# A recommendation MLP on one core: five gram units of chunk c+2 among layer 2 of chunk c, four spills and four gathers in place of one and sixteen

## The reference

```python
B, F, D = (2048, 27, 128)
dots = jnp.einsum('bfd,bgd->bfg', bottom_output, bottom_output)   # 27 x 27 per sample
pairs = dots[:, _TRIL_I, _TRIL_J]                                 # 351 of them
x = jnp.concatenate([bottom_mlp_output, pairs, pad], axis=1)      # 128 + 351 + 1 = 480
for w, b in ((w0, b0), (w1, b1), (w2, b2), (w3, b3)):             # 1024, 1024, 512, 256
    x = jax.nn.relu(x @ w.T + b)
return x @ w_out.T + b_out                                        # (2048, 1)
```

## Time and profile before

| | |
|---|---|
| median of 3 runs | 575.12 us (574.05 to 575.9) |
| profiled execution | 574.64 us, span of its profile 572.8 us |
| PE busy | 515.9 us (90%), 4073 matmuls |
| ACT, DVE, POOL busy | 334.4, 280.3, 262.5 us |
| DMA | 53.16 MB, mean 93 GB/s |
| SPq issues in the chain that ended last | 11%, spill 5%, gather's landing 2% |

### The profile page before, as it was taken

One profiled execution on the slowest core, in us unless ns is written; L12 is line 12 of the kernel. 1 busy time (PEld: TensorE's weight loads), 2 busy tenths in 40 slices (PEclk: granted clock), 3 DMA queues, 4 the chain that ended last, 5 costly groups with the idle time before them and its releaser, 6 DMA issues.

```text
span 572.8 us, 13768 instructions
## 1 busy us (share of the span) xinstructions
PE 515.9 (90%) x4073; PEld 506.0 (88%) x4073; DVE 280.3 (49%) x646; ACT 334.4 (58%) x844; POOL 262.5 (46%) x467
## 2 busy tenths in 40 slices
PE   6948977999999699969999699979999699979997
PEld 6938976999999699969999699969999699979996
DVE  2845875527751477326761377316761377412111
ACT  3635799527982389525992389625993289613112
POOL 2801266224773177513773167613774167623321
PEclk9987999899999799998999799998999799997999
DMA  9978572255722576127732577117732477110000
GB/s 243 281 259 197 135 117 46 79 92 79 112 35 78 85 119 109 62 40 121 116 50 75 84 116 114 62 32 122 117 57 74 77 126 110 46 41 1 1 1 1
DMA packets 263088, 53.16 MB, mean 93 GB/s; under 512 B 248950, under 2 KB 260246, under 8 KB 263062
## 3 DMA queue, kind: packets, MB, share of 16 engines
q1 hardware_dynamic: 262374, 52.66, 46.0%
q10 hardware_dynamic: 688, 0.16, 0.1%
HBM read 45.71 MB, written 7.09 MB: 92 GB/s over the span
## 4 chain that ended last, share of the span: by engine, by line
PE 66%; SPq 11%; DMA 8%; ACT 4%; issue 4%; POOL 3%; DVE 2%; ACTq 1%; POOLq 0%
PE acc L684 52%; SPq L378 11%; PE gram_ps L647 8%; DMA blocks<-grams 5%; ACT parts L775 3%; PE gram_ps L630 3%; DMA pairs<-blocks 2%; PE gram_ps L601 2%; ACT h_full L791 1%; PE turned_ps L606 1%; ACTq L378 1%; POOL parts L526 1%; POOL grams L533 1%; DMA early_rows<-in_r_bottom_output_dram 1%; DVE grams L888 1%
## 5 line engine op out<-in xcount | busy, mean ns | idle before, releaser
L684 PE MATMUL acc<-h_a,w_hi 128*128 128x256 f32 x1152 | 216.0, 286 | 1.4 <-POOL h_a L541 1.2
L684 PEld LDWEIGHTS acc<-h_a,w_hi 128*128 128x128 f32 x1152 | 180.2, 193 | 3.3 <-POOL h_a L541 2.8
L791 ACT ACTIVATE h_full<-acc,small_t 128x256 f32<-128x256 f32 x176 | 82.6, 473 | 148.7 <-PE acc L684 146.2
L541 POOL TENSOR_TENSOR h_a<-h_full,h_a 128x256 fp32r<-128x256 f32 x96 | 72.3, 753 | 204.0 <-DVE h_a L908 204.0
L684 PE MATMUL acc<-h_a,w_lo 128*128 128x256 f32 x576 | 163.2, 283 | 0.0
L775 ACT ACTIVATE parts<-gram_ps 27x216 f32<-27x216 f32 x448 | 152.4, 340 | 16.0 <-PE gram_ps L647 6.5
L684 PE MATMUL acc<-x,w_hi 128*128 128x256 f32 x512 | 109.9, 313 | 34.3 <-ACT h_full L791 25.8
L684 PEld LDWEIGHTS acc<-x,w_hi 128*128 128x128 f32 x512 | 91.3, 219 | 36.1 <-issue 22.8
L684 PEld LDWEIGHTS acc<-h_a,w_lo 128*128 128x128 f32 x576 | 110.8, 192 | 0.0
L684 PE MATMUL acc<-h_b,w_hi 128*128 128x256 f32 x512 | 94.2, 285 | 2.4 <-POOL h_b L541 2.4
L908 DVE CAST h_a<-h_full 128x256 fp32r<-128x256 f32 x96 | 29.2, 304 | 123.3 <-ACT h_full L791 123.3
(11 more groups left out here) (49 smaller groups left out, 390.0 us busy)
## 6 DMA issues: line engine op xcount, KB each, us to landing
rows<-in_r_bottom_output_dram SPq DMA_DIRECT2D x444, 64.0 KB, 2.0
blocks<-grams SPq DMA_DIRECT2D x8, 864.0 KB, 3.5
w_raw<-in_L_rec_w_dram SPq DMA_DIRECT2D x6, 1024.0 KB, 7.5
early_rows<-in_r_bottom_output_dram SPq DMA_DIRECT2D x12, 224.0 KB, 6.0
stage_pairs<-in_L_rec_w_dram SPq DMA_DIRECT2D x1, 1408.0 KB, 9.5
w_raw<-in_L_rec_w_dram SPq DMA_DIRECT2D x2, 512.0 KB, 8.9
mlp_rows<-r_bottom_mlp_output_dram SPq DMA_DIRECT2D x8, 128.0 KB, 2.2
pairs<-blocks SPq DMA_DIRECT2D x32, 31.5 KB
```

What stands on the lines that cost most here:

```text
L541: nc.gpsimd.tensor_tensor(h[:, m, 1, :], h_full[:, slot % 2, :], h[:, m, 0, :].bitcast(F32), ALU.subtract).then_inc(split_done, 1)
L684: last = nc.tensor.matmul(acc_slot(slot), weight(wp, layer, m, k), in_tile(layer, k, xp), start=(k == 0 and n == 0), stop=(k == K_TILES[la ...
L791: nc.scalar.activation(h_full[:, slot % 2, :], acc_slot(slot), ACT.Relu, bias=small_t[:, slot:slot + 1]).then_inc(drained, 1)
```

## The change

- A hook comes every 18 products instead of 15 in all chunks but chunk 0. A chunk's own list holds units 5 to 18 (14 hooks, the last at product 252) of chunk c+1, and in layer 2, at products 306, 324, 342, 360 and 378, hooks 0 to 4 of chunk c+2 (five row turns, four `xt`, two grams, one sum). Chunk 0 has these five at its hooks 49, 52, 55, 58 and 61. Chunk 6 has none ahead, so it leaves the loop and is written out.
- SP loads rows of chunk c+2's units 0 to 3 before the spill and of units 4 to 8 after the gather.
- `blocks` in DRAM is laid out by feature pair with a chunk's 256 samples in a row: the spill is four DMAs (one per sample group, 32 x 27 runs of 256 B), the gather four DMAs with runs of 1 KB.
- In the start-up SP issues two of the spills and ACT two, ahead of the bottom network's step; each issues two gathers.
- In chunk 0 the bottom network's products (k = 0) of tiles 0 to 5 come first, with tiles 2 to 5 in the banks of `turned_ps` and `gram_ps`. Their 18 products count for the hooks, so weight groups 9, 10 and 11 come among them. Tiles 4 and 5 wait for all eight groups of layer 0. Weight groups 9 to 24 use two banks of `gram_ps` instead of four.
- `weighted` has a tensor of its own, and two waits around `low_t` go.

```diff
-HOOK, FIRST_HOOK = 15, 6
+HOOK, FIRST_HOOK = 18, 6
+AHEAD, AHEAD_HOOK = 5, 49
-OUT_HOOK = 2
+OUT_HOOK, EARLY_TILES = 2, 6
...
-    steps.append(("mlp",))
+    steps += [("spill",), ("mlp",)]
...
+    for n in range(AHEAD):
+        hooks[AHEAD_HOOK + 3 * n] += unit_steps(n, 2)
     return hooks
...
+def hooks_of(now, ahead):
+    hooks = [unit_steps(n, 1) for n in range(AHEAD, UNIT_HOOKS)] if now else []
+    if ahead:
+        hooks += [[] for _ in range(len(hooks), 3 * TILE0[2] // HOOK)] + [unit_steps(n, 2) for n in range(AHEAD)]
+    return hooks
...
+    if first:
+        for m in range(EARLY_TILES):
+            products(0, m, 0, 1)
...
+            products(layer, m, 1 if first and layer == 0 and m < EARLY_TILES else 0, K_TILES[layer])
...
-        blocks = nc.dram_tensor("blocks", (GROUP, QUAD, FEATS, RUN), F32).ap()
+        blocks = nc.dram_tensor("blocks", (QUAD, FEATS, CHUNK), F32).ap()
...
+        def acc_slot(c, slot):
+            if isinstance(c, int) and c == 0 and 2 <= slot < EARLY_TILES:
+
+                return (turned_ps if slot < 4 else gram_ps)[:, slot - 2, 0:CHUNK]
             return acc[:, slot % ACC_RING, 0:CHUNK]
...
+            among = EARLY_TILES // 3 if BEFORE_CHUNK <= n < LATE_WEIGHTS else GRAM_RING * GRAM_BANKS
+            return gram_ps[:, n % among, :]
...
+        def spill_quad(engine, s):
+
+            engine.dma_start(blocks[:, :, s * RUN:(s + 1) * RUN], grams[QUAD * s:QUAD * (s + 1)]).then_inc(spilled, 16)
+
         def gather_piece(engine, f, nf, nk, q):
 
-            for s in range(GROUP):
-                src = bass.AP(blocks.tensor, (s * QUAD * FEATS + (FEATS + 1) * f + 1) * RUN,
-                              [[(FEATS + 1) * RUN, nf], [RUN, nk], [1, RUN]])
-                engine.dma_start(pairs[q % P:q % P + nf * nk, q // P, s * RUN:(s + 1) * RUN], src).then_inc(gathered[q // P], 16)
+            src = bass.AP(blocks.tensor, ((FEATS + 1) * f + 1) * CHUNK, [[(FEATS + 1) * CHUNK, nf], [CHUNK, nk], [1, CHUNK]])
+            engine.dma_start(pairs[q % P:q % P + nf * nk, q // P], src).then_inc(gathered[q // P], 16)
...
-                for u in range(ROWS_RING, UNITS):
+                start = isinstance(c, int) and c == 0
+                for u in range(ROWS_RING if start else ROWS_RING + AHEAD, UNITS):
                     load_rows(c + 1, u)
...
+                more = not (isinstance(c, int) and c == CHUNKS - 2)
+                if more:
+                    for u in range(ROWS_RING):
+                        load_rows(c + 2, u)
                 spill(c + 1)
                 gather(c + 1)
-                if not (isinstance(c, int) and c == CHUNKS - 2):
-                    for u in range(ROWS_RING):
+                if more:
+                    for u in range(ROWS_RING, ROWS_RING + AHEAD):
                         load_rows(c + 2, u)
...
+                elif BEFORE_CHUNK <= n < LATE_WEIGHTS:
+
+                    pe.wait_ge(w_done, max(n - 1, BEFORE_CHUNK))
...
-                        pe.wait_ge(w_done, groups_for(layer, m))
+                        pe.wait_ge(w_done, W0_GROUPS if layer == 0 and m >= 4 else groups_for(layer, m))
...
+                elif step[0] == "spill":
+                    act.wait_ge(grams_done, UNITS)
+                    act.wait_ge(early_moved, UNITS)
+                    for s in (2, 3):
+                        spill_quad(nc.scalar, s)
...
-                if u == 0 and not (isinstance(d, int) and d < 2):
-
-                    dve.wait_ge(summed_done, d - 1)
...
-                    dve.wait_ge(grams_done, (c + (1 if ends else 2)) * UNITS)
```

More of the change, by code:

```diff
@@ L111, with unit_steps @@
 assert len({q + i * d for _, n, q, d in ROW_RUNS for i in range(n)}) == PAIRS
-def unit_steps(n):
+def unit_steps(n, ahead):
     steps, g = [], n - 1 - XT_LAG
     if n < UNITS:
-        steps.append(("raw", n))
+        steps.append(("raw", ahead, n))
     if 1 <= n <= UNITS:
-        steps.append(("turn", n - 1))
+        steps.append(("turn", ahead, n - 1))
     if g >= 1:
-        steps.append(("sum", g - 1))
+        steps.append(("sum", ahead, g - 1))
     if g >= 0:
-        steps.append(("gram", g))
+        steps.append(("gram", ahead, g))
     if g == UNITS - 1:
-        steps.append(("sum", g))
+        steps.append(("sum", ahead, g))
     return steps
@@ L154, in first_hooks @@
     places = [FIRST_UNIT + 2 * i for i in range(4)] + [FIRST_UNIT + 8 + 4 * i // 3 for i in range(UNIT_HOOKS - 4)]
-    hooks = [[] for _ in range(LATE_HOOK + W_GROUPS - LATE_WEIGHTS)]
+    hooks = [[] for _ in range(3 * sum(K_TILES[n] * M_TILES[n] for n in range(3)) // FIRST_HOOK)]
     for n in range(BEFORE_CHUNK, LATE_WEIGHTS):
@@ L158, in first_hooks @@
     for u, place in enumerate(places):
-        hooks[place] += unit_steps(u)
+        hooks[place] += unit_steps(u, 1)
     for n in range(LATE_WEIGHTS, W_GROUPS):
@@ L162, in first_hooks, with chunk_steps, products @@
     assert places[-1] < LATE_HOOK
-    return hooks
-def chunk_steps(gram, first=False):
+    for n in range(AHEAD):
+        hooks[AHEAD_HOOK + 3 * n] += unit_steps(n, 2)
+    return hooks
+def hooks_of(now, ahead):
[3 more added lines that the diff above has]
+    return hooks
+def chunk_steps(now, ahead, first):
     steps, done = [], 0
-    hooks = first_hooks() if first else [unit_steps(u) for u in range(UNIT_HOOKS)] if gram else []
+    hooks = first_hooks() if first else hooks_of(now, ahead)
     every = FIRST_HOOK if first else HOOK
     hooks.reverse()
+    def products(layer, m, k, k1):
+        nonlocal done
+        while k < k1:
+            n = k1 - k
+            n = min(n, (every - done % every) // 3)
+            steps.append(("mm", layer, m, k, k + n))
+            k += n
+            done += 3 * n
+            if done % every == 0 and hooks:
+                steps.extend(hooks.pop())
+            if done == OUT_HOOK * every:
+                steps.append(("out",))
+    if first:
+        for m in range(EARLY_TILES):
+            products(0, m, 0, 1)
     for layer in range(3):
         for m in range(M_TILES[layer]):
-            if (layer, m) == (2, 2) and gram:
-                assert not hooks
+            if (layer, m) == (2, 2) and now:
                 steps.append(("mlp",))
[L180 to L193, removed]
+            products(layer, m, 1 if first and layer == 0 and m < EARLY_TILES else 0, K_TILES[layer])
+    assert not any(hooks)
+    if now:
         steps.append(("pairs",))
@@ L196, in chunk_steps, with steps_of @@
     return steps
+def steps_of(c):
+    fixed = isinstance(c, int)
+    return chunk_steps(not (fixed and c == CHUNKS - 1), not (fixed and c >= CHUNKS - 2), fixed and c == 0)
 def dlrm_program(nc, x, x_mlp, w0, b0, w1, b1, w2, b2, w3, b3, w_out, b_out, y):
@@ L544, in chunk @@
             def chunk(c):
-                ends = isinstance(c, int) and c == CHUNKS - 1
-                for step in chunk_steps(not ends, isinstance(c, int) and c == 0):
+                for step in steps_of(c):
                     if step[0] == "mm":
@@ L724, in _ @@
             chunk(0)
-            with pe.Fori(1, CHUNKS - 1) as c:
+            with pe.Fori(1, CHUNKS - 2) as c:
                 chunk(c)
+            chunk(CHUNKS - 2)
             chunk(CHUNKS - 1)
```

62 lines of the change are left out of this document (32 added, 30 removed).

## The result

| | before | changed |
|---|---|---|
| median | 574.89 us (574.05 to 575.9) | 532.16 us (530.62 to 536.04) |
| profiled execution, its span | 574.64, 572.8 us | 532.41, 530.6 us |
| chunk to chunk, chunks 2 to 5 | 64.9 us | 58.5 us |
| start of chunk 1 | 128.7 us | 126.5 us |

What follows compares the result with a forecast made beforehand. PE was taken as the bound nearly everywhere, standing still at chunk ends. 574.64 - 39.5 + 2.5 - 3.0 - 4.4 + 0.3 = 530.5, 531.0 on the median's footing; forecast range 526 to 536 (0.52).

Steps and rivals of the forecast that it cites:

- The handover: Ends of chunks 1 to 6: PE's pause and half clock both go, 6.6 us each, -39.5 us in all.
- the stalls' +0.5 and -0.5: Per chunk: layer 3's stall grows by 0.5 us, the stall and refill before layer 2 go, 0.5 us.
- The spill's price: Writing grams to DRAM at a chunk's end: 3.7 us transfer plus 1.3 is 5.0 us; range 3.5 to 8.8.
- The doubling: Spill, rival A: short writes at double price, 8.8 us, total 541.8; chance 0.28 together with rival of ACT-bound layers.
- Unit 4's rows: SP's queue behind the gather: rows land at 51.8, DVE must start by 54.2; 2.4 us slack, high spill 1.4 late.
- a sign of being wrong: Layer 2: DVE idle before raw with the rows as releaser would show the prediction wrong; no size given.
- Layer 3: Late last drain and split behind ACT's parts copies: stall about 0.7 us instead of 0.2, +2.5 us over five chunks.
- The stall between layers 1 and 2: PE's 0.41 us wait for POOL's last split of layer 1 goes with its refill, -3.0 us over six chunks.
- ACT held in layer 0: Layer 0 with full hooks: ACT needs 14.2 us for PE's 14.2; taken as 0, bounds 0 to 1 us each.
- The start-up: Before chunk 0's main work: PE restarts at 40.7 instead of 44.40, with three more products behind it, -4.4 us.
- The slower rival: Rival D, at spill: SP stands in it, gather and unit 4 wait; slower than before from 13.4 us; chance 0.04.
- The rival's formula: Spill of s us: each handover late by s - 7.4, start-up by s - 5.0; s = 14.3 gives 581.

Runs made afterwards that it cites:

- the gathers alone: The changed kernel with hooks 15 products apart and no units among layer 2, new layout and early products kept; 534.2 us, ratio 0.930.
- the drawing forward alone: The changed kernel with the old layout of `blocks`, one spill and 16 gathers; 571.7 us, ratio 0.995.
- unit 4's rows first: The changed kernel with SP issuing unit 4's rows of chunk c+2 between spill and gather, not in chunk 0; 532.0 us, ratio 0.928.
- four units: The changed kernel with four units among layer 2 instead of five; 530.0 us, ratio 0.925.
- hooks of 15: The changed kernel with hooks 15 products apart instead of 18, five units ahead kept; 534.3 us, ratio 0.930.
- the two spread-out versions: The changed kernel with four units ahead and chunk 0's units spaced three hooks in two units, or five in three; 525.1 us (0.914) and 526.2 us (0.916).

## Why the prediction was right, step by step

**The handover.** It was nearly the whole of the effect, and its size was right: 64.9 - 58.5 = 6.4 us a period against the forecast 6.6, in which the stalls' +0.5 and -0.5 cancel. After chunk 1's start the spans differ by 40.0 us; the forecast has 39.5 - 2.5 + 3.0 = 40.0, and 1.0 more for two units that move from chunk 6 to chunk 0 (two grams of 0.48). But the prediction credits the drawing forward (last gram after 252 products instead of 285) and the gathers together, and never asked what either would give alone. The runs did: the gathers alone close the pause, and the drawing forward alone gives 0.5%, because unit 4's rows then come late; where no unit needs them (chunk 6), it leaves 0.84 us. The prediction's own numbers would have said the former: 12 issues fewer at 0.74 are 8.9 us, the spill takes 1.5 more (3.2 as measured), and the pause was 4.3.

**The spill's price.** The term was too small, 5.0 for 6.7 us. The transfer was taken as 17 ns a run from the gather's reads; it is 19 ns, 4.1 us in all for 3.7. The doubling that the prediction read out of the 512 B rule of the Trainium skill ("DMA: Bandwidth & Descriptors") did not come: that case had a spill of 8.8 us. That short runs fall short of the long rows' rate the trace bears out, 19 ns against 10 for 256 B. The larger miss is what lies around the transfer, taken as 1.3 us from the old spill: seen in stretches of half a microsecond, about 1.1 us pass from the first issue to the first bytes, the transfers spread over 4.8 us, and 0.8 more pass until the gather is issued. The four issues did lie under the transfer, as the prediction has it: the engines are busy at 0.93 from 286 to 290. That cost nothing, as there was slack, except where it ran out: at unit 4's rows.

**Unit 4's rows.** Slack of 2.4 us was forecast; the longer spill took 1.7 of it, and the rest went in terms of 0.1 to 0.2 us each (gathers, landing, an earlier start of layer 2). DVE waited 1.12 us, which the prediction had named as a sign of being wrong, and began at 12.33 us of layer 2 (which starts at 285.92), where the prediction had 12.3 as the latest time that does no harm:

```profile
298.25 0.71 DVE L921 STREAM_TRANSPOSE raw<-rows 128x512 f32<-128x512 f32 x1 [1.12 <-DMA rows<-in_r_bottom_output_dram]
```

In chunk 1, whose spill took 7.45 us, it was later (DVE waited 1.77 us), and PE's stall was 1.02 us instead of 0.4. In the four others the forecast held by luck, with nothing to spare.

**Layer 3.** The walk through ACT's queue was close. It had the second parts copy at 12.1, the last drain at 13.5 and the pairs at 13.9 us of layer 2; the timeline of ACT has 12.16, 13.59 and 13.97:

```profile
298.08 1.41 ACT L817 ACTIVATE parts<-gram_ps 27x216 f32<-27x216 f32 x4 [0.24 <-PE gram_ps L688]
299.51 0.47 ACT L833 ACTIVATE h_full<-acc,small_t 128x256 f32<-128x256 f32 x1
299.89 1.02 ACT L843 ACTIVATE x<-pairs 128x256 fp32r<-128x256 f32 x3
```

About 0.7 us of stall was forecast, 0.20 + 0.44 measured. The stall between layers 1 and 2 went as forecast, and ACT held in layer 0. The forecast +2.5 and -3.0 nearly cancel, and the runs with no unit and with five ahead do not differ measurably (0.930 and 0.932, periods 58.6 and 58.5).

**The start-up** is the term that was wrong: -4.4 us forecast. PE's restart came at 41.04 (forecast 40.7), yet layer 1 of chunk 0 begins at 63.56 instead of 65.20. PE's rows with idle time, and stretches of 4 us (columns as above):

```profile
41.04 1.12 PE L642 MATMUL gram_ps<-ident,w_raw 128*128 128x128 f32 x4 [3.79 <-DVE ones L909]
...
46.34 1.11 PE L642 MATMUL gram_ps<-ident,w_raw 128*128 128x128 f32 x4 [0.77 <-DVE w_lo L912]
...
40.00:44.00 4.00, 2.96 (x15) 2.96 (x15) 1.18 (x3) 0.84 (x4) 0.00 (x0) 0.52 0.71 145
44.00:48.00 4.00, 3.23 (x16) 2.94 (x15) 2.49 (x5) 2.06 (x5) 0.00 (x0) 0.50 0.75 118
48.00:52.00 4.00, 4.00 (x27) 4.00 (x27) 1.77 (x4) 1.86 (x5) 0.74 (x1) 0.70 0.83 135
```

The failed step is that half clock costs the same wherever PE restarts. Before, PE began at 44.40 and reached full clock at about 50.3; now it begins 3.4 us earlier and still runs at half clock until about 50.3. The extra 3.4 us at half speed (half of the work of that time) give back 1.7. With a wait of 0.77 at the third weight group (`w_done`) and the restart 0.3 later than forecast that is 2.8, and 4.4 - 2.8 is the 1.6 us that layer 1 gained.

The rest of chunk 0 had luck. The kernel before lost 1.7 us to half clock after its wait of 2.1 us (granted clock 0.94 from 98 to 102 us, 0.63 from 102 to 106); the profiled execution of the changed kernel has the same wait and no such dip. Had it come at the same cost, chunk 1 would have started 0.5 us earlier than before, not 2.2 (two more units in chunk 0, 1.0 us, are in both figures). The prediction has no term for this. In another execution of the same start-up, that of the kernel with unit 4's rows first, full clock came back earlier:

```profile
40.00:44.00 4.00, 3.12 (x17) 3.12 (x18) 0.75 (x2) 0.49 (x3) 0.00 (x0) 0.68 0.82 175
44.00:48.00 4.00, 2.21 (x16) 1.92 (x16) 3.01 (x6) 2.41 (x6) 0.00 (x0) 0.90 0.69 108
```

In the nine profiled executions with this start-up and the same chunk 0 up to there (the changed kernel twice, gathers only, unit 4's rows first, four units, one spill, hooks of 15, the two spread-out versions), layer 1 of chunk 0 begins anywhere from 61.98 to 66.89 us. A spread of that size would account for medians of the same kernel 2.5 us apart, and it leaves the early products' worth open.

**The slower rival** was a real one: a single spill DMA is a spill of 17 us. The rival's formula, 6 (s - 7.4) = 58 us, would give 589; measured were 602. It left out the half clock that a pause brings back; at 2.1 us in six handovers, an estimate, that is 12.6 and makes up the difference. In the profiled execution the pause came as the rival's unit 4 (10.51 us in layer 3), five periods are 10 to 12.6 us longer than in the changed kernel, the last handover costs 9.4, and the start-up happened to be 3.0 longer.

## What to carry to other kernels

When a wait ends a chain of several links, work out what each link alone would save before paying for all of them: here twelve DMA issues fewer did what five units of careful reordering were also meant to do. Queue order is the other half: a step moved forward whose input stands behind a busy issue queue takes the pause with it. And a long pause of PE costs more than its length: the 4.2 us at a handover brought 2.1 us of half clock, so removing the pause gave back both, while after a wait of 2.1 us the half clock came in some executions only.

## What the runs showed of the hardware

- The same bytes in the same 3456 runs of 256 B took 6.7 us as four DMAs and 17.0 us as one; the one, with an outermost count of 4, used a quarter of the DMA engines' time. Four DMAs with an outermost count of 27 had a share of 0.61 while they ran, those with 32 had 0.93.
- A run of 256 B written to DRAM took 19 ns of engine time in three runs, against some 17 for one read (from a share of 0.11, so 16.5 to 18) and 10 for 256 B of a long row.
- After the start-up's idle time PE stayed at half clock for some 3 us in one execution (unit 4's rows first) and some 13 in another (hooks of 15) of the same start-up code, though both restarted at about 41 us; the latter had another wait of 2.1 us in between.
- The same wait of 2.1 us in chunk 0 was followed by half clock in 9 of 12 profiled executions, the kernel before among them, and by none in three, the changed kernel's two among them. The cost was 1.7 us in the kernel before and 3.0 with four units ahead. A pause of 0.84 us (old gather, chunk 6) was followed by full clock.
